# The last batch's expert sums read, added and stored in two halves

## What is computed

```python
h = tok(x)                    # 36 angles of each token id drive a 6-qubit circuit; 6 values -> 192
h = h + attn(layernorm(h))    # one head per batch of 512 tokens
h = h + ffn(layernorm(h))

def ffn(x):                   # 8 experts, each token takes its best 2
    gate_scores = x @ Wg
    topk_scores, topk_idx = top_k(gate_scores, 2)
    topk_probs = softmax(topk_scores)
    y = gelu(x @ W1[e] + b1[e]) @ W2[e] + b2[e]      # hidden width 384
    return sum of topk_probs * y over the two experts
```

## Time and profile before

| what | us |
|---|---|
| median of 3 runs | 297.91 |
| the runs | 297.30, 298.25, 297.91 |
| the profiled execution, its own time | 298.81 |
| its span in the trace | 297.1 |
| last read of `shares_out` issued | 287.50 |
| its data landed | 292.12 |
| DVE's four additions | 292.22 to 294.31 |
| last store issued | 294.34 |

### The profile page before, as it was taken

How to read it: one execution, slowest core, us unless ns; L and a number is a source line. 1 busy time by engine, 2 the same in 40 slices (tenths; PEclk the granted TensorE clock), 3 DMA queues, 4 the chain that set the end, 5 groups by cost and what they waited for, 6 DMA issues and landing times.

```text
span 297.1 us, 5762 instructions
## 1 busy us (share of the span) xinstructions
PE 210.9 (71%) x1552; PEld 149.9 (50%) x1552; DVE 174.9 (59%) x687; ACT 121.2 (41%) x292; POOL 210.6 (71%) x281
## 2 busy tenths in 40 slices
PE   0660796467964777887589689999999999896000
PEld 0550553122431434444255568788889899785000
DVE  4754999747799988685877857782221002552022
ACT  2002022136352332346442576667666667554000
POOL 5778785830899697877776776777777777777730
PEclk9999999555596655579755689999999999999555
DMA  7811004993000000000012221033333228977653
GB/s 168 269 21 15 1 5 133 396 338 129 2 0 2 4 7 15 11 13 17 12 32 53 58 38 20 24 89 91 96 101 88 78 79 281 364 259 228 176 164 138
DMA packets 25243, 29.86 MB, mean 101 GB/s; under 512 B 15098, under 2 KB 18673, under 8 KB 25019
## 3 DMA queue, kind: packets, MB, share of 16 engines
q1 hardware_dynamic: 18732, 21.54, 23.5%
q0 software_dynamic: 6480, 7.94, 8.6%
HBM read 14.13 MB, written 16.02 MB: 102 GB/s over the span
## 4 chain that ended last, share of the span: by engine, by line
PE 47%; DVE 20%; POOL 13%; issue 7%; ACT 7%; DMA 4%; POOLq 0%; DVEq 0%; SPq 0%; ACTq 0%
PE bank_b L2069 24%; PE bank_a L2057 6%; POOL circuit L527 5%; PE bank_b L1828 4%; POOL shares_out L755 3%; PE bank_a L1835 3%; DVE nmax L1176 3%; POOL rs L699 2%; PE bank_c L1847 2%; ACT prob L1566 2%; DMA angle_stages<-shares_out 2%; POOL routed L710 1%; PE bank_d L1931 1%; DVE circuit L868 1%; DMA shares_out<-circuit,up 1%
## 5 line engine op out<-in xcount | busy, mean ns | idle before, releaser
L755 POOL DMA_INDIRECT shares_out<-circuit,up x71 | 73.0, 1029 | 21.6 <-issue 14.9
L2069 PE MATMUL bank_b<-wide,up 128*128 x426 | 81.6, 340 | 3.2 <-ACT circuit L1705 2.0
L710 POOL DMA_INDIRECT routed<-rows,slot x64 | 63.3, 989 | 23.6 <-issue 19.0
L2069 PEld LDWEIGHTS bank_b<-wide,up 128*128 128x128 f32 x426 | 69.7, 194 | 10.7 <-issue 9.2
L1705 ACT ACTIVATE circuit<-bank_b,up 128x192 f32<-128x192 f32 x71 | 29.9, 421 | 25.8 <-PE bank_b L2069 24.7
L527 POOL DMA_INDIRECT circuit<-angles,ids x32 | 31.3, 979 | 10.8 <-issue 9.0
L1693 ACT ACTIVATE up<-bank_a 128x384 f32<-128x384 f32 x71 | 34.5, 489 | 7.0 <-PE bank_a L2057 6.9
L1835 PE MATMUL bank_a<-keys_t,wt 32*128 32x512 f32 x64 | 27.9, 959 | 4.7 <-DVE nmax L1176 3.0
L1828 PE MATMUL bank_b<-queries_t,keys_t 32*128 32x512 f32 x64 | 24.8, 855 | 6.2 <-ACT keys_t L1544 3.5
L1503 DVE TENSOR_TENSOR hres<-hres,prob 128x384 f32<-128x384 f32 x12 | 6.2, 555 | 36.6 <-DMA prob<-shares_out 36.5
L1176 DVE TENSOR_REDUCE nmax<-bank_a 128x2 f32<-128x1024 f32 x16 | 19.5, 1220 | 11.4 <-PE bank_a L1835 11.4
(11 more groups left out here) (431 smaller groups left out, 387.3 us busy)
## 6 DMA issues: line engine op xcount, KB each, us to landing
routed<-pad_rows SPq DMA_DIRECT2D x8, 528.0 KB, 5.2
out<-hres SPq DMA_DIRECT2D x8, 384.0 KB
wide<-down_w SPq DMA_DIRECT2D x1, 2304.0 KB, 11.8
prob<-shares_out SPq DMA_DIRECT2D x3, 768.0 KB
angle_stages<-shares_out SPq DMA_DIRECT2D x3, 768.0 KB, 6.9
up<-up_w SPq DMA_DIRECT2D x1, 1536.0 KB
form_p<-shares_out SPq DMA_DIRECT2D x2, 768.0 KB, 6.8
up<-routed SPq DMA_DIRECT2D x71, 16.0 KB, 1.7
```

Of the source, the lines that this page charges most:

```text
L710: pool.indirect_dma_start(out=routed, out_offset=bass.IndirectOffsetOnAxis(slot[:, b, k, j:j + 1], 0), in_=rows[:, b, k, j, :], in_offset=None
L755: pool.indirect_dma_start(out=shares_out, out_offset=bass.IndirectOffsetOnAxis(xb[:, m, DEST:DEST + 1].bitcast(I32), 0), in_=y[:, m % RESU ...
L2069: mm = pe.matmul(bank_b[:, m % 2, 0:D], hid[:, m % STEP, c * P:(c + 1) * P], wide_flat[:, bass.ds(first + c * D, D)], start=(c == 0), stop ...
```

## The change

Batches 0 to 6 are untouched. For batch 7 the read is issued as two DMAs, each of two tiles (128 x 2 x 384 floats, runs of 1536 bytes in place of 3072), on two new semaphores `last_in`. DVE adds k = 0 and then k = 1 to the first half, with a `join()` between, counts on `sum_done`, and does the same for the second half. SP issues both reads, then waits for the first half's sum and stores it (128 x 384 floats), then the second's. The last `load_sums` waited for `sum_done` of batch 4; the new reads don't. DVE's wait for `h2_copied` stands once ahead of both halves. The final wait counts 9 stores.

```diff
+        last_in = [sem(f"last_in{x}") for x in range(2)]
...
+            def load_last_half(x):
+
+                own = slice(x * TILES // 2 * D, (x + 1) * TILES // 2 * D)
+                b = BATCHES - 1
+                sp.dma_start(expert_sums[b % SUMS][:, :, own], shares_view[b][:, :, own]).then_inc(last_in[x], 16)
+
+            def store_last_half(x):
+                own = slice(x * TILES // 2 * D, (x + 1) * TILES // 2 * D)
+                b = BATCHES - 1
+                sp.wait_ge(sum_done, b + 1 + x)
+                sp.dma_start(out_view[b][:, own], hres[:, b, own]).then_inc(h2_out, 16)
...
             all_added(sp, BLOCKS)
-            load_sums(BATCHES - 1)
-            store(BATCHES - 1)
-            sp.wait_ge(h2_out, 16 * BATCHES)
+            for x in range(2):
+                load_last_half(x)
+            for x in range(2):
+                store_last_half(x)
+            sp.wait_ge(h2_out, 16 * (BATCHES + 1))
...
+            def add_last_half(x):
+                b = BATCHES - 1
+                dve.wait_ge(last_in[x], 16)
+                own = slice(x * TILES // 2 * D, (x + 1) * TILES // 2 * D)
+                sums = expert_sums[b % SUMS]
+                step(dve.tensor_tensor(hres[:, b, own], hres[:, b, own], sums[:, 0, own], ALU.add))
+                join()
+                dve.tensor_tensor(hres[:, b, own], hres[:, b, own], sums[:, 1, own], ALU.add).then_inc(sum_done, 1)
...
-            for b in range(BATCHES):
+            for b in range(BATCHES - 1):
                 add_experts(b)
+            dve.wait_ge(h2_copied, 2 * BATCHES)
+            for x in range(2):
+                add_last_half(x)
```

## The result

| | before | changed |
|---|---|---|
| median of 20 runs each, us | 298.73 | 296.29 |
| span of the profiled execution | 297.1 | 294.9 |
| last read's (first) issue to the span's end | 9.55 | 8.00 |
| first half landed, from that issue | | 3.39 |
| all data landed, from that issue | 4.62 | 4.37 |

The ratio of the two kernels is 0.9937, 95% interval 0.9915 to 0.9959: the change made the kernel faster, by 1.2 to 2.5 us.

A forecast was written before the change was run, and what follows sets the result against it. The kernel was taken to be bound at its end by batch 7's read, additions and store in a row; 0.71 us from read and additions plus 0.49 from the store, 1.20, took 297.91 to 296.7, range 296.1 to 298.0.

The forecast's parts named there:

- the likeliest case: Whole kernel: a gain of 0.9 to 1.5 us, median at 296.4 to 297.0; chance 0.64.
- The removed wait: SP ahead of the last read: no wait for batch 4's sum, so the first read is issued 0.06 us sooner.
- The last store: SP's last store moves half the bytes, 0.56 us in place of 1.05; gain 0.49.
- The rival of a store that doesn't shrink: Last store: a half moves as slowly as the whole, leaving only the additions' 0.71 us, 297.2; chance 0.12.
- The pair of additions: DVE, batch 7: two additions with a join take 1.15 us per half, starting 0.10 behind a landing.
- The first half's landing: First read of batch 7: in at 291.15 us, between bounds of 290.7 and 291.1 or so, engines finishing unevenly.
- the late bound: First read's landing: slowest engine works on its second half at full rate, 0.97 us before 292.06, or 291.1.
- the rival that they land together: Last reads: engines take packets of both in turn, both halves land about 292.35; gain 0.1 us, 297.8; chance 0.14.
- The second half's landing: Second read of batch 7: in at 292.35 us, between 292.06 without penalty and 292.53 with both.
- price per packet in the slow start: Start of the last read: if slow by packets, smaller packets cost 0.33 us more; about half was taken.
- Which wait ends last: DVE's second pair: starts at 292.45 us behind the second landing; a first half later than 291.3 would make DVE set it.
- The slower rival: Last read: a packet costs the same whatever its size, movement 3.15 us longer, time 300.1; chance 0.05.

The follow-up runs named there:

- e2: Changed kernel with the last read whole again, additions and stores still in halves; timed 0.9975 of the kernel before, end 9.39 us after the read's issue.
- e3: Changed kernel with one whole last store, reads and additions still in halves; timed 0.998 of the kernel before, end 8.78 us after the first issue.
- e5: Changed kernel with last read, additions and store in four pieces of one tile, runs of 768 bytes; timed 0.9946 of the kernel before.
- e0: The kernel before, unchanged, profiled once more; whole read landed at 4.57 us, end 9.50 after its issue.
- e10: Changed kernel with the two last reads of 64 partitions each, whole additions after both, one whole store; halves landed at 4.41 and 6.10 us.
- e9: Changed kernel with four last reads, k by halves, each addition waiting for its own; timed 0.99 of the kernel before, end 7.92 us after first issue.
- e7: Kernel before with the last read taking batch 0's rows in place of batch 7's; the read landed 4.21 us after its issue.
- e4: Changed kernel with the two last reads cut by k, runs of 3072 bytes; timed 0.9922 of the kernel before, end 7.76 us after first issue.

## Why the prediction was right, and which term was off

Forecast 296.7, measured 296.29, in the range; faster by over 0.3%, as the likeliest case had it. That the two lie only 0.4 apart is in part luck: the base of three runs was 0.82 us low, which makes the forecast too low, and the gain was put too small, which makes it too high. From 298.73 the same sum gives 297.5, still in the range. The gain was forecast at 1.20 us, 0.40%; the ratio says 0.41 to 0.85%, and the tails of the profiled executions say 1.6 (9.55 and 9.50 before, 8.00, 7.80 and 8.26 after: means 9.53 and 8.02, and 0.06 for the wait), which are 0.53%. Term by term:

- *The removed wait, 0.06*: right. SP's step from the last block's wait (286.85, 287.38 before) to the issue is 0.07 in place of 0.12.
- *The last store, 0.49*: right, 0.45 in the changed kernel. e2 and e3 isolate it: 1.87 for a half, 2.34 for a whole one. The rival of a store that doesn't shrink fell.
- *The pair of additions, 1.15, and the start 0.10 behind a landing*: right, 290.41 to 291.56, and 290.31 to 290.41.
- *The first half's landing, 291.15, 3.71 from the issue*: the late bound was taken; measured 3.39, 3.19 and 3.64. The first half was in 0.97 to 0.98 us ahead of the second in all three. That is the 393 KB / 406 GB/s = 0.97 of the late bound, and it disposes of the rival that they land together.
- *The second half's landing, 292.35, 4.91 from the issue*: this is the mis-sized term. Measured 4.37, 4.16 and 4.62, no later than whole reads (4.57 to 4.80). The two prices that I put on it, 7% for runs of 1536 bytes and half of a price per packet in the slow start, 0.29 together (292.35 - 292.06), did not make it land later. The price per packet in the slow start was wrong: the slow start did not grow with the number of packets (1.0 us in place of 1.5, and e5 with four times as many). The 7% is there in the packets, two of 65 ns for one of 121; it can't be found in the landings, since 0.14 us is less than they scatter.
- *Which wait ends last.* I had the second landing set the end by 0.05. With the second landing earlier, it was the first half's: the end of the additions is the first landing + 2.31 in the changed kernel three times and in e3. The forecast named this case ("DVE would set the start of the second pair") and gave it no weight; the two differ by under 0.1 us in the forecast and in the runs.

The additions and the read together gave 1.06 (6.78 to 5.72, means of two and three executions), where the forecast has 0.65 (0.71 less the 0.06 of the wait). Two things are in the 1.06. The additions end 1.33 to 1.34 behind the last landing in all three executions of the changed kernel, and 2.18 behind it before and in e0: that is 0.85 from work done under the second read (0.94 in the forecast). The other 0.2 is the last landing itself, 4.38 against 4.60 on average, and that this comes of the cut is not shown. So 0.85 + 0.45 + 0.06 = 1.36 us of the 1.6 are accounted for.

One sum of the forecast is off: 0.06 + 0.94 + 0.49 is 1.49, not about 1.4. Nothing else is worked out from it.

The slower rival, a price for each packet, was wrong by a wide margin: it needed 3.15 us more of reading, and five reads in halves show none. The Trainium skill, Perfetto Trace Analysis, section DMA Optimizations, has that small DMAs under 2 KB carry a significant overhead. The prediction took this for contiguous runs; each read here has 192 KB or more, so no run here tries the rule on DMAs that are small as a whole. Runs of 1536 and 768 bytes carried no such price (last landings 4.16 to 4.68 and 4.88, whole reads 4.57 to 4.80). What the same section says of splitting, that some of the pieces may start sooner and the task as a whole may complete sooner, agrees with the runs: 3.2 to 3.6 us to the first half in place of 4.6 to the whole, and 7.80 to 8.26 to the end in place of 9.50 and 9.55.

## What to carry to other kernels

Where a kernel ends with read, compute, store in a row and nothing beside them, two pieces hide a part of the computing under the second read (here 0.85 us of 2.09) and shorten the last store (here 1.88 in place of 2.33 us); cost it from the issue of the last read, since what lies ahead moves by more than the gain between executions. Look then at which landing ends last: once the compute of all pieces is longer than the rest of the transfer, the first piece's landing sets the end, and cutting the last one finer does not help the additions. In this kernel it paid to keep each read on all 128 partitions (e10), and by the tail three reads did better than four, whose transfer slackened in its middle (e9, e5); each of these is one profiled execution, and the timing has four reads ahead.

## What the runs showed of the hardware

- Two reads of 64 partitions moved 215 to 246 GB/s in their middle where the read of 128 partitions, with runs of the same 3072 bytes, moved 406, at about the same share of busy engines (e10). The cause wasn't tried.
- The last read starts slowly with batch 0's rows as with batch 7's: 0.12 and 0.14 MB in the first us (e7, before), while the store moved 369 GB/s in its second tenth of a us.
- The engines of one whole read finished 0.26 us apart with batch 0's rows (e7) and 0.97 to 1.25 apart with batch 7's (before, e0, e2).
- The time from the last scatter's start to the last read's issue was 3.12 to 3.21 us in ten executions in which the store of batch 6 was issued 0.4 us behind that scatter's start, and 2.58 to 2.67 in the four (e2, e4, e5, e9) in which it was issued ahead of it. All profiled executions of the two kernels that are compared here were in the first case, so it is no part of the tails; which case the other timed executions were in is not known, so some of what the timings have beyond the tails may be this. The cause is open.
